# A layernorm, attention and SwiGLU kernel: layernorm transposes moved to TensorE, weight conversions regrouped, layernorm steps spaced

## The reference

```python
x = x + layernorm(attn(layernorm(x), Mq, Mk, Mv))
x = x + layernorm(ffn(layernorm(x), w_gate, w_up, w_down))

def attn(x):                       # 8 heads, key size 64, value size 128
    q = (x @ Mq).reshape(B, H, C, K); k = (x @ Mk).reshape(B, H, C, K)
    v = (x @ Mv).reshape(B, H, C, V)
    att = softmax(q @ k^T / 8, axis=1)            # over the queries
    return (att viewed as (B, C, H, C)) @ v       # reshaped to (B, C, 1024)

def ffn(x):                        # int32 weights scaled by 1/127
    return (silu(x @ wg.T) * (x @ wu.T)) @ wd.T   # hidden size 3072
```

## Time and profile before

| quantity | value |
|---|---|
| device time, median of 3 runs | 1783.32 us (1781.84 to 1788.17) |
| device time of the profiled execution | 1786.53 us |
| its span on the slowest core (core 3) | 1785.1 us |
| spans of the eight cores | 1759.0 to 1785.1 us |
| DMA transposes in the projections | 12 |
| conversions into `gu_bf` from POOL | 10, and 4 hidden tiles in the FFN |

### The profile page before, as it was taken

How to read it: one execution, slowest core, us unless ns; L and a number is a source line. 1 busy time by engine, 2 the same in 40 slices (tenths; PEclk the granted TensorE clock), 3 DMA queues, 4 the chain that set the end, 5 groups by cost and what they waited for, 6 DMA issues and landing times.

```text
span 1785.1 us, 31871 instructions; the slowest of 8 cores (1759.0 to 1785.1 us)
## 1 busy us (share of the span) xinstructions
PE 1671.9 (94%) x10912; PEld 793.3 (44%) x10912; DVE 952.1 (53%) x2128; ACT 798.3 (45%) x967; POOL 124.9 (7%) x247
## 2 busy tenths in 40 slices
PE   5999779799989999999999999999999999999997
PEld 2444334344434444444444444444444444444443
DVE  3434457456445555556465655565656465655433
ACT  3443436455434454445444544554445444542111
POOL 2110001001101000100010001000100010001000
PEclk9999889899999999999999999999999999999999
DMA  9897999968973655365527553656356635552431
GB/s 196 182 201 164 203 216 177 208 175 211 200 213 112 200 153 157 98 201 154 160 84 211 153 174 84 186 165 190 83 171 171 196 80 173 148 166 57 153 95 48
DMA packets 224494, 284.17 MB, mean 159 GB/s; under 512 B 61008, under 2 KB 144976, under 8 KB 224336
## 3 DMA queue, kind: packets, MB, share of 16 engines
q1 hardware_dynamic: 212096, 259.06, 51.4%
q0 software_dynamic: 12240, 23.07, 9.2%
HBM read 257.95 MB, written 46.14 MB: 170 GB/s over the span
## 4 chain that ended last, share of the span: by engine, by line
PE 73%; DMA 9%; DVE 8%; issue 4%; ACT 3%; SPq 2%; POOL 1%; DVEq 0%; ACTq 0%; POOLq 0%
PE F L72 53%; PE O L72 13%; PE S L72 6%; DMA vt<-v_d 5%; ACT E L428 2%; DMA gu_bf<-wgu 1%; SPq L76 1%; SPq L79 1%; DMA xl<-x 1%; DVE x L508 1%; DVE bnB L229 1%; DVE bnB L230 1%; DVE bnB L484 1%; DMA wq<-mq 1%; DVE th L567 1%
## 5 line engine op out<-in xcount | busy, mean ns | idle before, releaser
L72 PE MATMUL F<-x2T,wgu 128*128 128x512 bf16 x3072 | 769.0, 382 | 23.3 <-DVE th L567 20.0
L428 ACT ACTIVATE E<-S 128x2048 bf16<-128x2048 f32 x256 | 480.7, 1878 | 639.3 <-PE S L72 639.3
L72 PEld LDWEIGHTS F<-x2T,wgu 128*128 128x128 bf16 x3072 | 260.9, 98 | 370.5 <-issue 169.8
L72 PE MATMUL F<-wd_sb,hT 128*128 128x512 bf16 x1536 | 364.7, 385 | 5.9 <-DMA wd_sb<-wd 5.9
L72 PE MATMUL O<-vt,E 128*128 128x128 bf16 x4096 | 314.8, 221 | 37.7 <-DVE vt L437 22.1
L72 PEld LDWEIGHTS O<-vt,E 128*128 128x128 bf16 x4096 | 272.8, 99 | 163.4 <-issue 52.4
L567 DVE SCALAR_TENSOR_TENSOR th<-th,F 128x512 f32<-128x512 f32 x192 | 132.1, 688 | 360.8 <-ACT th L561 360.6
L437 DVE TENSOR_SCALAR vt<-vt,rsx 128x512 bf16<-128x512 bf16 x512 | 178.8, 351 | 110.7 <-DMA vt<-v_d 64.4
L72 PEld LDWEIGHTS F<-wd_sb,hT 128*128 128x128 bf16 x1536 | 143.0, 99 | 177.3 <-issue 36.0
L72 PE MATMUL S<-qk 64*128 64x512 bf16 x1024 | 158.9, 390 | 0.8 <-ACT E L428 0.8
L561 ACT ACTIVATE th<-F 128x512 f32<-128x512 f32 x192 | 113.7, 592 | 72.9 <-PE F L72 72.7
(11 more groups left out here) (66 smaller groups left out, 870.9 us busy)
## 6 DMA issues: line engine op xcount, KB each, us to landing
wgu<-gu_bf SPq DMA_DIRECT2D x188, 512.0 KB, 4.4
vt<-v_d SPq DMA_DIRECT2D x512, 128.0 KB, 2.9
xl<-x SPq DMA_DIRECT2D x32, 512.0 KB, 9.8
x<-x SPq DMA_DIRECT2D x32, 512.0 KB, 5.8
out<-x SPq DMA_DIRECT2D x32, 512.0 KB, 2.9
gu_bf<-gu POOLq DMA_DIRECT2D x10, 1024.0 KB, 17.2
v_d<-vst SPq DMA_DIRECT2D x16, 512.0 KB, 6.7
qk<-qk_d SPq DMA_DIRECT2D x16, 512.0 KB, 5.5
```

The source lines that it names most:

```text
L72: "tensor", lambda t: t.matmul(out, lhsT, rhs, start=start, stop=stop),
L428: lambda s: s.activation(to, S[:, :], AF.Exp, scale=0.125, accum_out=accx[:, K % 16:K % 16 + 1]),
```

## The change

The transposes of blocks 5 to 7 also go to TensorE: `turn` for those tiles writes into a PSUM tile `tpF` that lies in the banks F0 and F1, taking the next bank of the `narrow` rotation between two projection units. Their scaling goes from DVE to ACT, and the copies out of PSUM alternate between ACT and DVE. The DMA transposes of the first layernorm are gone; those of the later one (`x2T`) stay. Twelve conversions run in the projections at new places (four instead of three in blocks 0 to 3, eight instead of seven after), and none in the FFN; `keep_wgu` is gone and the `wd` loads begin one pair earlier. `LEAD` is 9 instead of 8. The steps of the second and third layernorms are put down for each of the two tiles on its own, 2.6 planned us apart, with longer delays between them.

In the diff the removed lines of the old `half_stats` and `ln2` (L482 to L528, printed above), semaphore names, the removed `keep_wgu` call and two moved definitions are left out.

```diff
@@ -23,11 +23,10 @@
 NBLK = 8
 NKT = 256
-LEAD = 8.0
+LEAD = 9.0
 QUIET = 5
 MM = 0.216
 SPACE = 3.0
-CONV = 20
 ROW = 1088
@@ -208,12 +204,15 @@
     x1 += [sb(f"x1_{i}", [128, 1024], F32) for i in range(4, 8)]
     x2T += [sb("x2T1", [128, 8 * 512], BF16)]
+    def turned(name):
+        with ExitStack() as early:
+            return [early.enter_context(nc.psum_tensor(f"{name}{i}", [128, 1024], BF16)) for i in range(2)]
     O = [pt(f"O{i}", [128, 512], F32) for i in range(2)]
+    tpF = turned("tpF")
     F = [pt(f"F{i}", [128, 512], F32) for i in range(2)]
-    early = ExitStack()
-    tp = [early.enter_context(nc.psum_tensor(f"tp{i}", [128, 1024], BF16)) for i in range(2)]
-    early.close()
+    tp = turned("tp")
     S = pt("S", [128, 2048], F32)
     const_done = P.dve(lambda v: v.memset(mhalf[:, :], -0.5))
@@ -264,20 +263,13 @@
     def ln1(T):
-        s, blk, j = T % 4, T // 4, T % 4
+        s = T % 4
         ready = ln_stats(xl[s], bnA, mvA, vfA, rsA, s, EPS, xl_tok[T])
         busy = xn_read[T - 4] if T >= 4 else None
-        if blk < 5:
-            ready = ln_shift(mvA, rsA, nbA, s, ready)
+        ready = ln_shift(mvA, rsA, nbA, s, ready)
         def finish():
-            if blk < 5:
-                t = xn_tok[T] = ln_scale(xn[s], xl[s], rsA, nbA, s, ready, busy)
-            else:
-                t = ln_apply(xn[s], xl[s], mvA, rsA, s, ready, busy)
-                xn_read[T] = xnT_tok[T] = P.flip(xnT_part(T), xn[s][:, :], q_xnT[4 * (blk % 2) + j],
-                                                 t, proj_done[blk - 2])
-            xl_free[T] = t
+            t = xl_free[T] = xn_tok[T] = ln_scale(xn[s], xl[s], rsA, nbA, s, ready, busy)
             if T + 4 < 32:
                 load_x(T + 4, t, w_tok[0])
@@ -288,19 +280,28 @@
     def turn(T):
-        bank, dst = tp[T % 2], xnT_part(T)
+        dst = xnT_part(T)
+        if T < 20:
+            bank, free = tp[T % 2], tp_free.get(T - 2)
+        else:
+            name, _ = next_bank(narrow)
+            bank, free = tpF[int(name[1])], bank_free[name]
         for dt in range(8):
-            first = [xn_tok[T], tp_free.get(T - 2), ident_done] if dt == 0 else ()
+            first = [xn_tok[T], free, ident_done] if dt == 0 else ()
             done = P.put("tensor", lambda e, dt=dt: e.transpose(
                 bank[:, 128 * dt:128 * (dt + 1)], xn[T % 4][:, 128 * dt:128 * (dt + 1)],
                 ident[:, :]), first, "c_tensor" if dt == 7 else None)
         xn_read[T] = done
         over = proj_done[T // 4 - 2] if T >= 8 else None
-        if T in (2, 3):
+        if T in (2, 3) or T >= 20 and T % 2:
             t = P.dve(lambda v: v.tensor_copy(dst, bank[:, :]), done, over)
         else:
             t = P.act(lambda a: a.copy(dst, bank[:, :]), done, over)
-        xnT_tok[T] = tp_free[T] = t
+        xnT_tok[T] = t
+        if T < 20:
+            tp_free[T] = t
+        else:
+            bank_free[name] = t
     evac_n = [0]
@@ -314,19 +315,21 @@
     bank_free = {}
     qk_stored, v_stored = {}, {}
+    wide = [(f"{n}{i}", t[i][:, :]) for n, t in (("O", O), ("F", F)) for i in range(2)]
+    narrow = wide[2:]
+    rotation = [0]
+    def next_bank(banks):
+        rotation[0] += 1
+        return banks[rotation[0] % len(banks)]
     def proj_units(blk, banks):
         par = blk % 2
         xT = xnT[par]
         qk_ev, v_ev = {}, {}
-        turn = [0]
-        def bank():
-            turn[0] += 1
-            return banks[turn[0] % len(banks)]
         def group(lhs, rhs, ready):
-            name, ap = bank()
+            name, ap = next_bank(banks)
             done = None
             for dt in range(8):
                 first = [bank_free.get(name), *ready] if dt == 0 else ()
@@ -474,58 +477,48 @@
             ev.append(t)
         o_free[:] = ev
         if Q % 4 == 3:
...
+            for d in range(2):
+                P.later(1.5 + 2.6 * d, lambda d=d: half_stats(G, c, d))
+    def half_stats(G, c, d):
+        u, s = 2 * G + c, 2 * (G % 2) + d
+        o, y = 12 * s + 6 * c, y2[u % 3]
+        t = P.dve(lambda v: v.bn_stats(bnB[:, o:o + 6], y[:, 512 * d:512 * (d + 1)]), y2_tok[u, d])
         if c:
...
+            ln2(G, d, t)
+    def ln2(G, d, stats):
+        blk, n, s = G // 2, 2 * G + d, 2 * (G % 2) + d
+        xt, jj = x1[n % 8], 2 * (G % 2) + d
+        shift = ln_shift(mvB, rsB, nbB, s, ln_rstd(bnB, mvB, vfB, rsB, s, EPS, stats))
+        halves = [y2[(2 * G + c) % 3][:, 512 * d:512 * (d + 1)] for c in range(2)]
+        def scale():
+            t = [P.act(lambda e, part=part: e.activation(
+                part, part, AF.Identity, bias=nbB[:, s:s + 1], scale=rsB[:, s:s + 1]), shift)
+                for part in halves]
+            P.later(1.3, lambda: residual(t))
+        def residual(scaled):
             for c in range(2):
...
+                t = y2_tok[2 * G + c, d] = P.dve(lambda v, c=c: v.tensor_tensor(
+                    xt[:, 512 * c:512 * (c + 1)], xt[:, 512 * c:512 * (c + 1)], halves[c], AL.add),
+                    scaled[c], x1_tok[n])
+            P.later(4.0, lambda: stats3(t))
+        def stats3(t):
+            ready = ln_stats(xt, bnB, mvB, vfB, rsB, 4 + s, EPS, t)
+            P.later(4.0, lambda: flip(ready))
+        def flip(ready):
+            t = ln_apply(x2[d], xt, mvB, rsB, 4 + s, ready, x2T_tok.get(n - 2))
+            dst = bass.AP(x2T[blk % 2], 128 * jj, [[4096, 128], [512, 8], [1, 128]])
+            x2T_tok[n] = P.flip(dst, x2[d][:, :], q_x2T[4 * (blk % 2) + jj], t,
+                                *([up_done[blk - 2]] if blk >= 2 else ramp_idle if blk else ()))
+        P.later(2.2, scale)
     up_done = {}
@@ -534,18 +527,9 @@
     def load_wgu(i):
         ht = i % NHT
-        spill = [conv_tok[i - 4]] if CONV <= i - 4 < NHT else []
-        if CONV <= i < NHT:
-            wgu_tok[i] = P.dma("gpsimd", wgu[i % 4][:, :], gu_hbm[ht, :, :], q_wgc[i % 4],
-                               wgu_read[i - 4], *spill)
-        else:
-            wgu_tok[i] = P.dma("sync", bass.AP(wgu[i % 4], 0, [[2048, 128], [1024, 2], [1, 1024]]), gu_bf[ht, :, :, 0:1024], q_wgu[i % 4],
-                               conv_tok[ht], wgu_read.get(i - 4), *spill, *(xl_idle if i < 4 else ()))
-    def keep_wgu(i):
-        conv_tok[i] = P.dma("sync", gu_bf[i, :, :, 0:1024],
-                            bass.AP(wgu[i % 4], 0, [[2048, 128], [1024, 2], [1, 1024]]), q_keep[i], wgu_tok[i])
+        wgu_tok[i] = P.dma("sync", bass.AP(wgu[i % 4], 0, [[2048, 128], [1024, 2], [1, 1024]]),
+                           gu_bf[ht, :, :, 0:1024], q_wgu[i % 4],
+                           conv_tok[ht], *([wgu_read[i - 4]] if i >= 4 else xl_idle))
     def gate_unit(n, ht):
         i = NHT * n + ht
@@ -704,8 +683,8 @@
     norm_at = {0: 4, 1: 5, 2: 6, 3: 7, 13: 8, 14: 9, 15: 10, 16: 11,
                25: 12, 26: 13, 27: 14, 28: 15, 34: 16, 36: 17, 38: 18, 40: 19}
     turn_at = {24: 8, 25: 9, 26: 10, 27: 11, 33: 12, 34: 13, 35: 14, 36: 15, 49: 16, 51: 17, 53: 18, 55: 19}
-    early_conv = {22: 0, 34: 1, 46: 2}
-    later_conv = {(4, 8): 3, (5, 0): 4, (5, 8): 5, (6, 0): 6, (6, 8): 7, (7, 0): 8, (7, 6): 9}
+    early_conv = {22: 0, 32: 1, 42: 2, 52: 3}
+    later_conv = {(4, 6): 4, (4, 14): 5, (5, 6): 6, (5, 14): 7, (6, 6): 8, (6, 14): 9, (7, 4): 10, (7, 10): 11}
     for u, unit in enumerate(first + rest):
         if u == 8:
             for T in range(4, 8):
@@ -736,8 +715,10 @@
     P.beside = beside_proj
     for blk in range(4, 8):
         for u, unit in enumerate(proj_units(blk, narrow)):
-            if u % 3 == 0 and u < 12 and blk < 7:
-                ln1(4 * (blk + 1) + u // 3)
+            if blk < 7 and u in (0, 2, 4, 6):
+                ln1(4 * (blk + 1) + u // 2)
+            if blk < 7 and u in (5, 8, 11, 14):
+                turn(4 * (blk + 1) + u // 3 - 1)
             unit()
             if (blk, u) in later_conv:
                 convert(later_conv[blk, u], ("c_tensor", P.count["c_tensor"]))
@@ -758,7 +739,7 @@
     first_block = {}
     for c in range(12):
-        first_block[7 + 4 * c // 3] = lambda *w, c=c: load_wd(c, *w)
+        first_block[6 + 4 * c // 3] = lambda *w, c=c: load_wd(c, *w)
     UNITS = 2 * NHT + 16
     main = [0.0]
```

More of the change, by code:

```diff
@@ L145, in build @@
     q_xl = [P.sem(f"q_xl{i}") for i in range(4)]
-    q_xnT = [P.sem(f"q_xnT{i}") for i in range(8)]
     q_w = [P.sem(f"q_w{i}") for i in range(3)]
@@ L153, in build @@
     q_x2T = [P.sem(f"q_x2T{i}") for i in range(8)]
-    q_conv = [P.sem(f"q_conv{i}") for i in range(CONV // 2)]
-    q_keep = [P.sem(f"q_keep{i}") for i in range(NHT)]
+    q_conv = [P.sem(f"q_conv{i}") for i in range(NHT // 2)]
     q_wgu = [P.sem(f"q_wgu{i}") for i in range(4)]
-    q_wgc = [P.sem(f"q_wgc{i}") for i in range(4)]
     q_wd = P.sem("q_wd")
@@ L476, in unload @@
         if Q % 4 == 3:
-            P.later(1.5, lambda: half_stats(G, c))
-    def half_stats(G, c):
-        u, a = 2 * G + c, 2 * (G % 2)
-        y = y2[u % 3]
-        for d in range(2):
```

(44 more changed lines are left out.)

## The result

The changed kernel took 1758.7 us (median of 4 runs, 1753.96 to 2016.47) against 1785.7 for the kernel before on the same chip; the ratio is 0.984, with a 95% interval of 0.980 to 0.988. It is faster, by about 28 us, and not by the 73 that I forecast; 1710 and the range up to 1748 missed it. Some executions on a chip are disturbed as a whole and stretch a median or a maximum, the ratios given here leave them out, so I compare by ratios.

What follows compares the result with a forecast made beforehand. TensorE (busy 94%) bounds the kernel, with 113.2 us idle and 44.6 lost to clock. Terms 43 + 11 + 20.4 - 1 = 73.4 us gained gave 1710 us; own range 1695 to 1727, with rivals 1685 to 1748.

Steps and rivals of the forecast that it cites:

- The projections: Blocks 5 to 7, transposes moved to TensorE: 36.8 us less 6.4 less 10, 20.4 gained, bounds -5 and 32.
- Of the other 39.8 I keep 3 for small waits: Projections outside block 7's part: of 39.8 us lost to idle and clock, 36.8 come back and 3 stay.
- rival 1: DMA-bound projections: engines full, v and x loads late instead of transposes; projections gain 0, total 1730; chance 0.18.
- The 17.7 us that I kept for block 7: Block 7, 320 to 360 us: 10.9 idle and 6.8 of clock, all expected to stay.
- My ceiling from the DMA work: Projections: 201 us of DMA work stay in a stretch forecast at 213, so the gain can't pass 32 us.
- The cost side: Projections: twelve TensorE transposes add 6.4 us of PE work, and waits for their banks 10 us, bounded by 0 and 25.
- The spaced steps: Second and third layernorm steps spaced along the FFN: 28 us of waits plus 15 of clock, 43 gained, bounds 19 and 52.
- I keep 6 us of idle: FFN gate phase: of 34 us waiting on DVE, 6 stay because DVE falls behind up to a microsecond once a group.
- The clock's part: FFN clock loss: 15 us back from spaced steps, bounds 5 and 18, and 3.4 at the wd wait.
- rivals 1 and 2: The second: DVE short in the window, not misordered; several small stalls, clock still falls; gain 18, total 1735; chance 0.14.
- The first FFN block: End of that block: the 5.9 us wd wait goes with 3.4 of clock and small waits; 11 gained, bounds 5 and 12.
- Blocks 0 to 3: Early projections: one conversion more, 7.1 us of DMA time, charged as 1 us lost, between 0 and 7.

Runs made afterwards that it cites:

- experiment 3: Changed kernel without the eight conversions of blocks 4 to 7 (weights reused, so another output); ratio 0.972 to the kernel before.
- 9: Changed kernel with second tile's layernorm steps 5.0 planned us after the first's, plus six late conversions moved to level DMA load; ratio 0.972 to the kernel before.
- 6: Changed kernel with the eight 1 MB conversions of blocks 4 to 7 cut into sixteen of 0.5 MB, spread evenly; ratio 0.984 to the kernel before.
- experiment 2: Changed kernel with the DMA transposes of blocks 5 to 7 put back; ratio 0.992 to the kernel before, head 381.5.
- Experiment 5: Changed kernel with second tile's layernorm steps 5.0 instead of 2.6 planned us after the first's; ratio 0.976 to the kernel before, 0.975 in its second run.
- the third row: Changed kernel with conversions and wd loads placed as before, TensorE transposes kept, run side by side on one chip; head 367.4, rest 1388.6.

## Why the prediction was wrong

The order of things was right: PE's idle time and its clock are what can be given back, and the change is faster. Two terms carried the miss.

**The projections (forecast 20.4 gained, measured 4 to 7 us lost).** The step that failed is "Of the other 39.8 I keep 3 for small waits". Idle time and clock before block 7's weight loads went only from 38.4 to 33.6 us on the slowest core. I gave the late v tiles to the DMA transposes' hold of the SP queue, and held against rival 1 that such holds "are seen at transposes alone". In the changed kernel a plain v load of 128 KB held the queue for 8.5 us:

```profile
194.22 8.47 SPq L75 DMA_DIRECT2D vt<-v_d  x1
```

The longest hold of this kind is 3.5 to 8.5 us on its eight cores. It was already 3.8 to 7.2 in the kernel before, and it is at most 2.7 without the late conversions. The 17.7 us that I kept for block 7 did stay (16.4 on the slowest core by the table's cut), and 13.5 of the 19.8 us of v waits lie in block 7. The longest chain before the stall at 211, in the changed kernel:

```profile
188.50 17.73 DMA vt<-v_d
...
210.56 0.60 DVE kst L312
...
211.30 1.01 PE F L71 x2
```

A v tile load took 17.7 us to land. DVE waited for it in front of the scaling, and the copy out of a projection bank stood behind: that is 4.5 of the new row's 9.9 us. Another 3.8 stand behind six statistics of 0.7 us in DVE's list, and are there without the late conversions too (3.0 to 3.8 in experiment 3):

```profile
274.67 1.02 PE L71 MATMUL F<-xnT,wk 128*128 128x512 bf16 x4 [3.82 <-DVE rsx L439]
```

What the runs put in the step's place: the conversions delay the v tiles, whoever transposes. Without them 9 us less are lost before block 7's weight loads and 14 less behind (experiment 3); where they stand decides the second part (9); halving them changes next to nothing (6). Transposes by DMA add to it, by 5 to 12 us of head beside the new conversions, so what the change removed was real, and the conversions' share of the waits was left. Rival 1 had this, at 1730 and 0.18. My ceiling from the DMA work (201 us in 213) was right as a sum (0.86 of 238.1, or 205, measured) and wrong as a test, since a mean over the stretch doesn't tell when a v tile is late. I also read the stretch from the slowest core alone: 38.4 us are lost there before the weight loads and 28.4 on the median core, and the `xnT` wait is 11.8 us there and 3.2 to 7.2 on the other seven.

The cost side held. The transposes into `tpF` kept PE busy 7.8 us (6.4 forecast) at 0.6 each:

```profile
L291 PE MATMUL tpF<-ident,xn x96: 219/219/314, 159.4 to 303.1; 128*128 128x128 bf16 x96
L299 ACT COPY xnT<-tpF x6: 992/1008/1012, 160.1 to 295.9; 128x1024 bf16<-128x1024 bf16 x6
L297 DVE COPY xnT<-tpF x6: 684/692/693, 167.6 to 303.4; 128x1024 bf16<-128x1024 bf16 x6
```

and the waits of projection units behind copies rose by some 7 to 8 us on the median core (2.2 to 3.2 on the cores before, 7.9 to 13.0 after) for a forecast of 10. The road was in part another: the two largest are the 4.5 and 3.8 above, and of the larger ones only a wait of 1.5 us at 169 has an exp, with a scaling, in front of the copy.

**The spaced steps (forecast 43 gained, measured 23).** The step that failed is "I keep 6 us of idle", with ACT's wait set at 0 ("I set 0, the 0.8 us times 16 groups (13) as a loss if ACT waits with a tanh behind it"). The copy out of O behaved as forecast, 14.7 to 0.8. The gate multiply did not: 20.2 stand there, 16.9 of them behind ACT. I had found DVE's bursts small enough once spaced, and behind DVE's own list only 3.3 of the 20.2 are left. But ACT has one gap, the 2.6 us behind a tanh, and two scalings 2.6 planned us apart can't both be in it. Experiment 5 showed it, by moving the second tile by one pair: 20 us became 3. The clock's part was near: outside of the projections the kernel before lost 44.6 - 18.7 = 25.9 us, the changed one 26.3 - 14.3 = 12.0 (the 14.3 are 0.06 of 238.1), so 13.9 came back for a forecast of 15 + 3.4.

Either miss alone was inside the range (1730 and 1735 by rivals 1 and 2); the two together were not. As measured the parts give 23 + 8 - 4 = 27 us, for 28 in all.

**The first FFN block (forecast 11, measured 8).** From the third row to the changed kernel the rest falls from 1388.6 to 1380.7. Right in kind; `wd` is no longer waited for, while 3.1 us of waiting for `wgu` are new on the slowest core.

**Blocks 0 to 3 (1 us).** PE was busy without a gap and at clock 1.00 from 60 to 135 in the changed kernel too; nothing was lost.

Rule and row on the transposes: the Trainium skill (Advanced Engine Details and Errata, X-Bar Transpose (TRN2)) has transposing DMAs as fast as regular ones. The runs don't bear this out in effect: putting twelve DMA transposes of 0.25 MB back beside the new conversions made the head 5 us later side by side and 12 in experiment 2, though TensorE's transposes and the waits behind their copies, some 15 us, went away with it.

Experiment 5's rest fell by 9 us for 17 us less waiting on the gate multiply, because other waits grew: PE's idle time in the rest fell by just 9 (33.2 to 24.0 on the median core). In its second run S matmuls wait 5.2 to 5.3 us behind an exp on every core, where the changed kernel has no such row, and the first `x2T` is late by 5.3 on the slowest (1.4 to 4.2 on the others). Open is which of the moved steps makes them.

```profile
PE F L71 <- DMA x2T<-x: 5.3, 1, 5.3
PE S L71 <- ACT E L431: 5.3, 6, 1.3
```

## What to carry to other kernels

A wait that names an engine names the last link. Before crediting its removal to an edit, ask what each instruction ahead of it on that engine was waiting for, and in a list that is executed in order look at every engine that the moved steps touch, not the one that the wait names: a step fits where the neighbour has its gap, and half a period away it doesn't. And a mean DMA share says little: here a stall of 10 us stood in windows of 0.8, and levelling the shares helped only in one place. Look for what was issued right in front of the load that came late, and move bulk transfers away from there before making them smaller. Read the waits on all cores, too; here the slowest one had lost a third more than the median in the stretch in question.

## What the runs showed of the hardware

How late a v tile lands in the median doesn't tell how long PE waits. Halving the conversions brought the median landing to 6.0 to 8.6 us by core (7.2 to 9.1 with whole ones), and the v waits stayed (16 to 27 us, against 18 to 21). With TensorE transposes and the old conversions it is 5.7 us on the slowest core, with 19 to 29 us of v waits on the cores. A few late tiles make the wait.

Issuing a plain load can hold SP's queue like a transpose does: 8.5 us for one v tile, against a median of 0.32.

The clock answers to like stalls in different ways. In the FFN of the changed kernel six stalls of 2.16 to 2.32 us came alike, one in each of blocks 1 to 6. In the 20 us windows around them the granted clock was 0.91 three times and 1.00 three times (PE: busy, clock, DMA share, GB/s; one of each kind):

```profile
615.00:635.00 20.00, 17.84 (x117) 0.91 0.50 125
795.00:815.00 20.00, 16.87 (x125) 1.00 0.52 121
```

So a stall of this size costs 2.2 us, or 4.0 with the clock (0.09 of 20 us more), and an estimate for one alone has to carry both.
